# Scaling gathered rows by ScalarE instead of VectorE in the second stage of a four-layer graph network

## What is computed

```python
h = jnp.maximum(_layernorm(x, axis=-1), 0.0)
x = x + _L1_gnn_ref(h, src, dst, L1_gnn_fc_w, L1_gnn_fc_b)
...
def _L1_gnn_ref(feat, src, dst, fc_w, fc_b):
    out_deg = jnp.clip(jax.ops.segment_sum(ones, src, num_segments=N_NODES), 1.0)
    in_deg = jnp.clip(jax.ops.segment_sum(ones, dst, num_segments=N_NODES), 1.0)
    h = feat @ fc_w.T + fc_b
    h = h * (out_deg ** (-0.5))[:, None]
    agg = jax.ops.segment_sum(h[src], dst, num_segments=N_NODES)
    rst = agg * (in_deg ** (-0.5))[:, None]
    rst = rst + feat
    return rst
```

## Time and profile before

| | |
|---|---|
| median of 3 runs | 2442.53 us (2442.11 to 2446.15) |
| the profiled execution | span 2443.7 us |
| PE busy | 1785.7 us, 73% |
| VectorE busy | 1845.2 us, 76% |
| ScalarE busy | 1377.4 us, 56% |
| GpSimd busy | 1781.6 us, 73% |
| mean granted clock of TensorE | 0.877 of full speed |

### The profile page before, as it was taken

How to read it: one execution, slowest core, us unless ns; L and a number is a source line. 1 busy time by engine, 2 the same in 40 slices (tenths; PEclk the granted TensorE clock), 3 DMA queues, 4 the chain that set the end, 5 groups by cost and what they waited for, 6 DMA issues and landing times.

```text
span 2443.7 us, 26381 instructions
## 1 busy us (share of the span) xinstructions
PE 1785.7 (73%) x6414; PEld 872.1 (36%) x6414; DVE 1845.2 (76%) x3016; ACT 1377.4 (56%) x3086; POOL 1781.6 (73%) x1776
## 2 busy tenths in 40 slices
PE   3888888874998588878999878868999788860000
PEld 1333333322444244334444334434444344430000
DVE  6999998746888488986999688886999799960000
ACT  2766676632887365546888655546888666620000
POOL 6777777776777777736777577756777577777776
PEclk9999999986999799978999888988999899975555
DMA  3344443224776354434444356654444455440000
GB/s 71 90 124 129 127 123 97 71 75 132 233 240 216 115 182 128 133 115 107 129 131 130 102 167 188 184 170 115 128 130 129 112 139 136 129 133 22 23 21 20
DMA packets 223229, 302.24 MB, mean 124 GB/s; under 512 B 78896, under 2 KB 85165, under 8 KB 222952
## 3 DMA queue, kind: packets, MB, share of 16 engines
q1 hardware_dynamic: 166632, 249.64, 31.3%
q0 software_dynamic: 56448, 50.92, 11.6%
HBM read 156.13 MB, written 144.91 MB: 123 GB/s over the span
## 4 chain that ended last, share of the span: by engine, by line
DVE 23%; POOL 21%; issue 14%; PE 10%; ACT 6%; DMA 1%; DVEq 0%; POOLq 0%; SPq 0%; ACTq 0%
POOL mn_ring L529 13%; POOL out_dram L1889 8%; DVE node_h L1407 5%; PE bank L1197 5%; DVE mn_total L1581 4%; DVE node_x L1431 2%; DVE node_h L1452 1%; DVE mn_ring L1566 1%; ACT node_square L1326 1%; DVE node_mean L1414 1%; DVE mn_scaled L1597 1%; ACT node_std L1310 1%; PE bank L1206 1%; PE bank L1201 1%; PE bank L1191 1%
## 5 line engine op out<-in xcount | busy, mean ns | idle before, releaser
L529 POOL DMA_INDIRECT mn_ring<-slot_rows,addr_i x980 | 976.8, 997 | 390.4 <-issue 295.5
L1197 PE MATMUL bank<-node_x,center 128*128 128x512 f32 x492 | 250.8, 624 | 97.0 <-DVE node_h L1407 92.7
L1326 ACT ACTIVATE node_square<-bank 128x512 f32<-128x512 f32 x246 | 145.9, 593 | 222.6 <-PE bank L1197 222.6
L1201 PE MATMUL bank<-node_square,mean 128*128 128x512 f32 x492 | 265.5, 622 | 3.4 <-ACT node_std L1305 2.7
L1206 PE MATMUL bank<-node_h,wconv 128*128 128x512 f32 x492 | 266.1, 624 | 0.3 <-DVE mn_sums L1719 0.3
L529 POOL DMA_INDIRECT found<-node_table,look_i x196 | 209.7, 1070 | 74.9 <-issue 62.8
L529 POOL DMA_INDIRECT xin<-in_x_dram,src_i x192 | 195.2, 1017 | 64.3 <-issue 57.6
L529 POOL DMA_INDIRECT xin<-in_x_dram,dst_i x192 | 196.5, 1023 | 58.5 <-issue 58.5
L1889 POOL DMA_INDIRECT out_dram<-keep,scat_i x196 | 193.1, 985 | 62.5 <-issue 62.5
L1211 PE MATMUL bank<-node_act,wconv 128*128 128x512 f32 x442 | 230.9, 605 | 1.9 <-ACT node_act L1320 1.9
L1320 ACT ACTIVATE node_act<-bank,bias 128x512 f32<-128x512 f32 x246 | 170.5, 693 | 86.0 <-PE bank L1206 86.0
(11 more groups left out here) (337 smaller groups left out, 3807.0 us busy)
## 6 DMA issues: line engine op xcount, KB each, us to landing
out_dram<-node_rows SPq DMA_DIRECT2D x98, 256.0 KB, 3.4
mn_rin<-res SPq DMA_DIRECT2D x96, 256.0 KB, 3.6
slot_rows<-node_rows SPq DMA_DIRECT2D x96, 256.0 KB, 2.1
slot_rows<-keep SPq DMA_DIRECT2D x96, 256.0 KB, 2.3
mn_fcol<-f_rows SPq DMA_DIRECT2D x192, 128.0 KB
res<-mn_x SPq DMA_DIRECT2D x72, 256.0 KB, 3.0
node_x_in<-in_x_dram SPq DMA_DIRECT2D x64, 256.0 KB, 3.0
mn_ring<-slot_rows,addr_i POOLq DMA_INDIRECT x980
```

The lines of the kernel that those rows point to most:

```text
L529: return eng.indirect_dma_start(out=dest, out_offset=None, in_=table, in_offset=bass.IndirectOffsetOnAxis(ap=index, axis=0))
L1197: pe.matmul(bank[i][:, :], C["center"][:, :], src, start=True, stop=True).then_inc(s["centered"][i], 1)
L1201: pe.matmul(bank[4][:, :], C["mean"][:, :], nd.square[:, i - 1, :], start=True, stop=True) \
L1326: act.activation(nd.square[:, i - 1, :], bank[i][:, :], ACT.Square).then_inc(s["squared"][i], 1)
```

## The change

The multiply of the gathered rows in stage B leaves VectorE. ScalarE does it, one instruction of 128x64 per tile with the tile's column of `osc` as scale, in place in `ring`. Group 0 is done at the head of step (B, 0); group g + 1 is done in step (B, g) behind `deviation` of group g - 1 and ahead of `rest`. `gs` is raised by the last piece.

```diff
@@ gather_sum (VectorE)
+                    if st == "B":
+                        return
                     v.wait_ge(s["fetched"][k], gathers(i))
-                    if st == "B":
-                        v.tensor_tensor(rows3(ring[:, k, :], g), rows3(ring[:, k, :], g), scale(C["osc"], g), ALU.mult) \
-                            .then_inc(s["gs"], 1)
-                    else:
-                        if st in "DF":
-                            v.wait_ge(s["row"], i - 2 * n + 1)
-                        v.tensor_tensor(here, here, of_group(keep, g), ALU.add).then_inc(s["gs"], 1)
+                    if st in "DF":
+                        v.wait_ge(s["row"], i - 2 * n + 1)
+                    v.tensor_tensor(here, here, of_group(keep, g), ALU.add).then_inc(s["gs"], 1)
@@ ScalarE
+                def weigh_rows(g):
+                    i = at("B", g)
+                    k = i % R
+                    if g == 0:
+                        act.wait_ge(s["late"], mark["osc"])
+                    act.wait_ge(s["fetched"][k], gathers(i))
+                    for j in range(tiles(g)):
+                        t = 2 * GP * g + j
+                        last = act.activation(ring[:, k, j * F:j * F + F], ring[:, k, j * F:j * F + F], ACT.Copy,
+                                              scale=C["osc"][:, t:t + 1])
+                    last.then_inc(s["gs"], 1)
+
                 for i, (st, g) in enumerate(order):
+                    if (st, g) == ("B", 0):
+                        weigh_rows(0)
...
                     if st in NORMS and g > 0:
                         deviation(norm_at(st, g - 1), g - 1)
+                    if st == "B" and g < n - 1:
+                        weigh_rows(g + 1)
```

## The result

The changed kernel took 2481.3 us (median, 2480.8 to 2482.7), the kernel before 2442.4 us: ratio 1.0148, 95% interval 1.0136 to 1.0160. It is 38.9 us slower; 2480 had been forecast.

The account below looks back on a forecast made before the run. VectorE, busy 203 of 230 us, was read as bound by the order inside a step, waiting for ScalarE's square. Terms 4.9 + 8.1 + 8.1 + 8.9 + 7.6 = 37.6 us gave 2480, forecast 2470 to 2491, wider range 2461 to 2500.

Parts of the forecast that it names:

- The removal: VectorE's multiply L1561: 16.8 us of work removed, worth nothing on the path, since L1648 still waits for ScalarE's square.
- B: Time by which eight new ScalarE multiplies move back the instruction behind them: 2.0 us, bounds 1.66 and 2.7.
- Tick steps, output units: Nine steps with a node tick: second L1407 waits for ScalarE's delayed L1310, 0.9 us late each, 8.1 us.
- With local units: Six tick steps where four local copies also queue behind the block: 1.35 us late each, 8.1 us.
- Steps without tick: Seven steps without node tick: PE's turn L1918 waits for the multiplied rows, next scan 1.27 us late, 8.9 us.
- Steps behind a tickless one: Five tick steps (4, 8, 11, 15, 18): PE's queue behind late L1918 delays product and norm's exp by 1.53, 7.6 us.
- The start: First two blocks of the stage: L1918 2.9 us late for group 0, 4.9 us late altogether after block 1.
- Rival 1: VectorE is the bound and ScalarE's block vanishes in idle time: all 16.8 us come back, 2426; chance 0.05.
- rival 3: The tail's slack covers the block in tick steps; only start and tickless steps pay: 21.4 us, 2464; chance 0.12.
- rival 2: The square's wait stays and ScalarE's slack takes the block everywhere: no change, 2442.5; chance 0.04.
- Rival 4: ScalarE's pieces do not overlap, so the block takes 2.7 us: 2497; chance 0.09.
- Rival 5: New waits in tick steps lower PE's clock, doubling some 3 us of PE work: 18 us more, 2498; chance 0.05.

Follow-up runs that it names:

- e1: Kernel before with VectorE's multiply L1561 cut from 512 columns to 8, nothing added on ScalarE; 2446.6 against 2447.1 us, ratio 0.9998.
- e3: Changed kernel with 2 pieces of 256 columns per group in place of 8 of 64; 2457.8 us, 10.8 over the kernel before, ratio 1.0038.
- e7: Changed kernel with ScalarE's block two groups ahead, in tick steps behind L1378, groups 0 and 1 around stage A's last ticks; 2448.5 against 2447.1 us, ratio 1.0005.
- e2: Kernel before, VectorE's multiply kept, plus 8 ScalarE instructions per group at the same queue place, result unused; 2461.1 us, 14.0 more, ratio 1.0057.
- e5: Changed kernel with 16 pieces of 32 columns per group in place of 8 of 64; 2520.4 us, 75.7 over the kernel before, ratio 1.0304.
- e11: Kernel before with ScalarE's blocks two groups ahead, L1662 and L1665 moved into VectorE's waits, SyncE's norm stores one step later; 2431.7 against 2445.7 us, ratio 0.9943.

## Why the prediction was right, and where its parts were off

1. **The removal is worth nothing.** Right, by the mechanism given: L1646 starts with the end of the square, with a wait of 0.7 before it, and e1 shows it alone (ratio 0.9998).
2. **The block.** B was taken as 2.0; it is 1.91 (998.55 to 1000.46), a piece takes 0.332 (0.34 forecast) and starts 0.24 behind the one ahead. What I built from L800, L1310 and L2012 was 0.01 too long per piece. L2030, which the prediction read as agreeing with 0.24 by its average of 0.22, does not: its pieces take 0.325, so eight in 1.75 start 0.20 apart. They overlap by 0.12, the new ones by 0.09. The Trainium skill, ScalarE: Activation LUTs, section What ACT_TABLE_LOAD costs, has figures from which I estimate 0.333 for a piece and 0.24 from start to start, and the trace agrees (0.332 and 0.24).
3. **Tick steps, output units.** B - 1.1 was the rule; 1.91 - 1.1 = 0.81, measured 0.80 (0.5 in step 9, which took 13.26 in the kernel before, not 11.9). With local units 1.35 was forecast; steps 2 and 5 cost 1.1 and step 6 0.7. Why steps 6 and 9 pay less was not followed up.
4. **Steps without tick.** 1.27 forecast, 1.14 measured in step 14: from the start of L2012 to the scan 3.32 (1023.91 to 1027.23), where it was 2.18. The block was done 0.09 sooner than taken, and the turn followed it by 0.06, not 0.14.
5. **Steps behind a tickless one.** This term was mis-sized: 1.53 each, 7.6 in all, forecast; measured 0.4, 0.4 and 0.0 in steps 11, 15 and 18, 0.7 in step 8, 1.9 in step 4 (each less what a step of its kind costs behind a tick step), 3.4 in all. The start of the norm's exp against its scan says the same: it moved by 0.37, 0.39, 0.01, 0.65 and 1.91 in these five, and by no more than 0.02 in the steps behind a tick step. The step of the reasoning that failed is that PE's queue behind the late L1918 would have no gap and take as long as before, as read from steps 14 and 15. It took less in step 15: L1201's pair 1.13 in place of 1.91, the granted clock of the step 0.90 in place of 0.86. In steps 4 and 8 PE had waited 0.36 and 1.18 us for the scan ahead of the product, which takes up a part of the 1.53; in step 4 the clock then fell from 1.00 to 0.83 and L1201's pair took 1.92 in place of 1.02. e3 shows that the same place can cost 1.6. Step 1 also stands behind a tickless step and was left out of the term: its exp moved by 1.23, and it cost 2.4, 1.3 more than steps 2 and 5. With it the term is 4.6.
6. **The start.** Scan 0 was 2.8 late as forecast (2.9), scan 1 another 3.8 in place of 2.0. There PE went the other way: behind a pause of 2.59 us that it did not have before, its granted clock was 0.60 over step 0 (1.00 before), and the product's two pairs took 1.68 and 2.07 where they had taken 1.12 each. The fifth rival, PE's clock, was looked for in every tick step; in those behind another tick step, such as 12, it does not occur (1.00), but it occurs at the start and in steps 1 and 4 (0.87 and 0.83, both 1.00 before).
7. **The total.** The stage lost 31.6 against 37.6 forecast: the start cost 1.7 more than forecast, and tick steps, tickless steps and those behind a tickless one each less. The measured 38.9 is nearer to the forecast than the stage is: 3.6 us stood ahead of the stage in the profiled run, and the profiled execution of the kernel before was itself a long one. The changed kernel's profiled execution took 2480.8 for a span of 2479.0, so 1.8 lie around a span; for the span of 2443.7 that makes 2445.5, which is 3.0 above the median, not the 1.2 that I read off. The direction and the size of the mechanisms are shown; the agreement to a microsecond is luck.

Rival 1 (faster) and rival 3 (half) are refuted by e7 and e2, rival 2 (no change) by the result. Rival 4 (pieces without overlap) is refuted by eight pieces in 2.00. Rival 5 is refuted in its size (18 us more), not in its mechanism, see 6.

## What to carry to other kernels

Taking work off the busiest engine brings nothing where that work fills a wait: look at what releases the engine's next instruction, and if that is another engine's end, look for work of the path to put into the gap (here 11 us gained in place of 0). What is added to a less busy engine is priced by what stands right behind it in that engine's queue and by who waits for its result, not by the engine's idle time: the same eight instructions cost 39 us in one place and nothing some 3 us further down the step, two groups ahead. An operation that is moved takes its store with it, and a store that becomes ready later holds up all that follows on its queue.

## What the runs showed of the hardware

- ScalarE (e5, changed kernel, e3), 128 partitions, SBUF to SBUF, float32, per-partition scale: 0.306 us for 32 columns, 0.332 for 64, 0.492 for 256; 8 pieces of 64 take 2.00 in a row, 16 of 32 take 3.48, 2 of 256 take 0.89. From start to start that is 0.21, 0.24 and 0.40.
- ScalarE with a PSUM source, otherwise the same form (L2030, kernel before): 0.325 for 64 columns, 8 pieces in 1.75, so 0.20 from start to start.
- TensorE's clock in step 11, behind a pause: after a wait of 4.44 us in the changed kernel it was back at the higher level for L1201 (1.07), after one of 3.33 us in e3 it was not (1.90). Both steps lost 1.2, though the block of e3 takes 0.89 and costs nothing by its place in the queue.
- GpSimd, indirect gathers of 128 rows of 64 float32 (kernel before and e11): 1.25 us from issue to issue at best, 1.33 on average.
